# A decoder kernel on one core: setup joined to the main program, and in the 32-head stage the projections moved ahead of the scores and half of the softmax sums done by GpSimd

## The reference

```python
def _L3_attn_ref(x, w_qkv, w_out, b_out, ln_gamma, ln_beta):   # HEADS = 32, DIM_HEAD = 32
    qkv = (x @ w_qkv).reshape(b, n, 3, HEADS, DIM_HEAD).transpose(2, 0, 3, 1, 4)
    q, k, v = (qkv[0], qkv[1], qkv[2])
    dots = jnp.einsum('bhnd,bhmd->bhnm', q, k) * 32 ** (-0.5)
    attn = jax.nn.softmax(dots, axis=-1)
    out = jnp.einsum('bhnm,bhmd->bhnd', attn, v).transpose(0, 2, 1, 3).reshape(b, n, 1024)
    out = out @ w_out + b_out           # then a layer norm with ln_gamma and ln_beta
```

## Time and profile before

| What | Value |
|---|---|
| median of three runs | 1448.85 us |
| the profiled execution, its time | 1460.55 us |
| its span, from first to last instruction | 1458.7 us |
| mean granted TensorE clock | 0.927 |
| PE busy | 1230.4 us (84%) |
| DVE busy | 918.5 us (63%) |
| ACT busy | 649.7 us (45%) |
| POOL busy | 170.3 us (12%) |
| chain that ended last, PE's share | 70% |

### The profile page before, as it was taken

The page is one execution under the profiler, slowest core; times in us unless marked ns, Lnnn a source line. Parts: engine busy times, 40 slices in busy tenths (PEclk is TensorE's granted clock), DMA queues, the critical chain, the costliest instruction groups (busy, mean ns, idle before and its releaser), DMA issues.

```text
span 1458.7 us, 27476 instructions
## 1 busy us (share of the span) xinstructions
PE 1230.4 (84%) x10752; PEld 858.3 (59%) x10752; DVE 918.5 (63%) x2432; ACT 649.7 (45%) x1253; POOL 170.3 (12%) x242
## 2 busy tenths in 40 slices
PE   2489999999999999997888998787879986898751
PEld 1356766776676767775555676454556564556530
DVE  2463453536786878877775877975875446544557
ACT  2134345445544554456543446442436643554320
POOL 3221021102200200020000120000030001000011
PEclk9589999999999999998997999997989999999975
DMA  7001110111021102110000010000000000000000
GB/s 273 1 1 44 44 30 17 57 51 52 10 64 51 52 1 73 30 30 1 2 1 1 2 37 1 1 2 1 2 1 2 1 2 2 1 2 1 2 0 29
DMA packets 23143, 35.59 MB, mean 24 GB/s; under 512 B 4568, under 2 KB 12904, under 8 KB 22760
## 3 DMA queue, kind: packets, MB, share of 16 engines
q1 hardware_dynamic: 23016, 33.83, 7.5%
HBM read 32.77 MB, written 1.05 MB: 23 GB/s over the span
## 4 chain that ended last, share of the span: by engine, by line
PE 70%; DVE 13%; ACT 8%; issue 6%; POOL 1%; DVEq 0%; ACTq 0%; POOLq 0%
PE banks L1187 12%; PE banks L1171 11%; PE banks L1925 5%; PE banks L1938 4%; PE banks L1946 3%; DVE arena L2066 2%; ACT XALL L535 2%; PE banks L1967 2%; PE banks L923 2%; PE banks L897 2%; PE banks L545 2%; PE banks L1920 2%; PE banks L661 2%; PE banks L1886 1%; PE banks L937 1%
## 5 line engine op out<-in xcount | busy, mean ns | idle before, releaser
L2066 DVE TENSOR_REDUCE arena<-banks 128x4 f32<-128x1024 f32 x128 | 151.1, 1219 | 106.1 <-PE banks L1902 106.0
L1187 PEld LDWEIGHTS banks<-WE,arena 128*128 128x128 f32 x1536 | 180.0, 192 | 24.4 <-issue 23.3
L1231 ACT ACTIVATE arena<-banks,BC 128x512 f32<-128x512 f32 x192 | 130.5, 688 | 120.2 <-PE banks L1171 119.9
L1187 PE MATMUL banks<-WE,arena 128*128 128x128 f32 x1536 | 182.3, 276 | 0.0
L1171 PE MATMUL banks<-XT,WE 128*128 128x512 f32 x384 | 179.0, 602 | 0.0
L2044 ACT ACTIVATE arena<-banks 128x1024 f32<-128x1024 f32 x128 | 126.4, 1022 | 112.2 <-PE banks L1925 111.5
L1271 DVE SCALAR_TENSOR_TENSOR R<-banks,arena,R 128x128 f32<-128x128 f32 x256 | 71.9, 343 | 111.2 <-PE banks L1187 110.9
L1925 PE MATMUL banks<-arena 32*128 32x256 f32 x1024 | 112.7, 396 | 0.0
L579 ACT COPY arena<-banks 128x512 f32<-128x512 f32 x108 | 61.3, 591 | 115.2 <-PE banks L574 35.8
L1171 PEld LDWEIGHTS banks<-XT,WE 128*128 128x128 f32 x384 | 69.2, 192 | 69.1 <-issue 67.6
L1741 DVE TENSOR_TENSOR arena<-arena 128x512 f32<-128x512 f32 x144 | 100.8, 700 | 3.8
(11 more groups left out here) (305 smaller groups left out, 2149.4 us busy)
## 6 DMA issues: line engine op xcount, KB each, us to landing
WE<-in_weights SPq DMA_DIRECT2D x64, 256.0 KB, 2.9
WE<-in_weights SPq DMA_DIRECT2D x64, 128.0 KB, 2.2
WS<-in_weights SPq DMA_DIRECT2D x1, 2368.0 KB, 13.2
RW<-in_rows SPq DMA_DIRECT2D x1, 1032.0 KB
XALL<-in_x SPq DMA_DIRECT2D x4, 256.0 KB, 10.8
out_dram<-arena SPq DMA_DIRECT2D x4, 256.0 KB, 2.3
WS<-in_weights SPq DMA_DIRECT2D x1, 900.0 KB, 7.9
WS<-in_weights SPq DMA_DIRECT2D x1, 645.0 KB, 8.0
```

What stands on the lines that cost most here:

```text
L1187: ins = PE.matmul(v[:, tile(t)], self.HT[:, e % 2, j, tile(t)], self.W[:, (8 * i + e) % RING, 1, j], start=j == 0, stop=j == self.J - 1)
L1231: A.activation(self.HT[:, e % 2, j], psum.view(f"{self.L}.h{i}.{e}.{j}"), ACT.Relu, bias=bcol(self.p + "_b1", e * self.J + j))\
L2066: V.tensor_reduce(big.mx[:, 2 * pair:2 * pair + 2], v, AX.X, ALU.max, negate=True).then_inc(dve.read(f"big.m{i}.{n}.{pair}"), 1)
```

## The change

1. The setup functions become `setup_sp`, `setup_pool`, `setup_act` and `setup_dve`, called at the head of the main block's programs. What the end of the first block assured is now waited for by semaphores: PE waits for `setup_step` 23 before its first transposes and for `heads_made` 15 before `x0`, POOL for `heads_made` 15 after its own setup, DVE for `setup_step` 31 before the first decay product. The first weight DMA (645 KB) is split: the four weights of the first projections alone under `w_loaded[0]`, the rest under `small_loaded`.
2. In `big`, project(n+2) stands ahead of scores(n) and not project(n+3) behind values(n-1); ACT's copies(n+2) stand ahead of the exponentials of group n.
3. GpSimd adds the exponentials of the second key block to those of the first, in place, for groups 0 to 14 of each chunk: 60 additions of 128x1024 elements. PE's sum matmuls (`sums`) of those groups then cover one key block. They stand one slot later than before, between project(n+2) and scores(n) as sums(n-2), and wait for the addition. The addition itself waits for the product with v, which reads what it overwrites. Group 15 keeps both key blocks. Inversion, spreading and output of the first batch come one slot later.
4. `TURNS` is a new string. The lengths of the stages are the same.

```diff
 TURNS = (
-    "00000000000000010010101000101011011010101010112021022010012202021021200121010021101202101201320323031121023012"
+    "00000000000000010010011000101011101010101010110212102200212012120021210010210200101202101203102011021211230203"
...
-        with nc.Block(no_gpsimd_drain=True) as block:
-            @block.sync
-            def _(sp):
-                sp.dma_start(XALL[:, 0:4], x[:, 0:4]).then_inc(x_loaded[0], 16)
-                load_group(sp, 0)
+        def setup_sp(sp):
+            sp.dma_start(XALL[:, 0:4], x[:, 0:4]).then_inc(x_loaded[0], 16)
+            sp.dma_start(WS[:, 0:4 * D], weights[:, 0:4 * D]).then_inc(w_loaded[0], 16)
+            sp.dma_start(WS[:, 4 * D:GROUP_AT[1]], weights[:, 4 * D:GROUP_AT[1]]).then_inc(small_loaded, 16)
...
@@ big_pe
-                if n % 8 == 0:
-                    psum.take(pe, f"big.sum{i}.{n // 8}")
-                v = psum.view(f"big.sum{i}.{n // 8}")
-                for kt in range(2):
-                    for h in range(4):
-                        ins = PE.matmul(v[32 * h:32 * h + 32, 0:S], group_column[:, n % 8].rearrange("p a c -> p (a c)"),
-                                        big.E[:, n % 2, h, kt, :], start=n % 8 == 0 and kt == 0,
-                                        stop=n % 8 == 7 and kt == 1, skip_group_check=True)
...
+            def sums(n):
+                b, g = divmod(n, 8)
+                added = n < GROUPS - 1
+                if added:
+                    pe.wait_ge(sig("big.added"), (GROUPS - 1) * i + n + 1)
+                if g == 0:
+                    psum.take(pe, f"big.sum{i}.{b}")
+                v = psum.view(f"big.sum{i}.{b}")
+                for kt in range(1 if added else 2):
+                    for h in range(4):
+                        ins = PE.matmul(v[32 * h:32 * h + 32, 0:S], group_column[:, g].rearrange("p a c -> p (a c)"),
+                                        big.E[:, n % 2, h, kt, :], start=g == 0, stop=g == 7 and (added or kt == 1),
+                                        skip_group_check=True)
...
             for n in range(GROUPS + 1):
                 if n + 1 < GROUPS:
                     maxima(n + 1)
+                if n + 2 < GROUPS:
+                    project(n + 2)
+                if n >= 2:
+                    sums(n - 2)
                 if n < GROUPS:
                     scores(n)
                 if n >= 1:
                     values(n - 1)
...
-                if n + 3 < GROUPS:
-                    project(n + 3)
                 if n + 1 < GROUPS:
                     shifts(n + 1)
@@ big_act
             for n in range(GROUPS + 1):
+                if n + 2 < GROUPS:
+                    copies(n + 2)
...
-                if n + 3 < GROUPS:
-                    copies(n + 3)
@@ big_pool
-            yield from idle(GROUPS + 2)
+            for n in range(GROUPS + 1):
+                if 1 <= n < GROUPS:
+                    pool.eng.wait_ge(*psum.made(f"big.o{i}.{n - 1}"))
+                    E = big.E[:, (n - 1) % 2]
+                    G.tensor_tensor(E[:, :, 0], E[:, :, 0], E[:, :, 1], ALU.add).then_inc(pool.flag("big.added"), 1)
+                yield
+            yield
@@ main block
             @block.tensor
             def _(eng):
+                eng.wait_ge(setup_step, 23)
                 run(0, lambda i: eng)
...
             @block.vector
             def _(eng):
+                setup_dve(eng)
```

More of the change, by code:

```diff
@@ new lines, in setup_sp @@
+        def setup_sp(sp):
+            sp.dma_start(XALL[:, 0:4], x[:, 0:4]).then_inc(x_loaded[0], 16)
+            sp.dma_start(WS[:, 0:4 * D], weights[:, 0:4 * D]).then_inc(w_loaded[0], 16)
+            sp.dma_start(WS[:, 4 * D:GROUP_AT[1]], weights[:, 4 * D:GROUP_AT[1]]).then_inc(small_loaded, 16)
+            sp.dma_start(BC[:], bcols).then_inc(small_loaded, 16)
+            sp.dma_start(RW[:], rows.partition_broadcast(P)).then_inc(small_loaded, 16)
+            sp.dma_start(B2[:], b2s.rearrange("l e d -> e l d")).then_inc(small_loaded, 16)
+            sp.dma_start(CD[:], ctx_d).then_inc(loaded, 16)
+            sp.dma_start(KEEP0[:], keep0.partition_broadcast(P)).then_inc(loaded, 16)
+            sp.dma_start(KEEP3[:], keep3.partition_broadcast(P)).then_inc(loaded, 16)
+            for half in range(2):
+                keys = slice(64 * half, 64 * half + 64)
+                with nc.allow_non_contiguous_dma(reason="the masks, keys on partitions"):
+                    sp.dma_start(KEEPC0[keys], keep0.rearrange("b k -> k b")).then_inc(loaded, 16)
+                    sp.dma_start(KEEPC3[keys], keep3.rearrange("b k -> k b")).then_inc(loaded, 16)
+            sp.dma_start(XALL[:, 4:8], x[:, 4:8]).then_inc(x_loaded[1], 16)
+            for e in range(RING):
+                load_expert(sp, 0, e)
+            load_group(sp, 3)
+            for e in range(RING):
+                load_expert(sp, 1, e)
+            load_group(sp, 5)
+            load_group(sp, 6)
+            for i in range(2, CHUNKS):
+                sp.dma_start(XALL[:, 4 * i:4 * i + 4], x[:, 4 * i:4 * i + 4]).then_inc(x_loaded[i], 16)
@@ L738, in ret_dve @@
                 if k < PAIRS:
+                    if i == 0 and k == 0:
+                        dve.eng.wait_ge(setup_step, 31)
                     dve.eng.wait_ge(*psum.made(f"ret.s{i}.{k}"))
@@ L841, in pe @@
                 L = self.L
+                pe.wait_ge(heads_made, 15)
                 pe.wait_ge(loaded, LOADS * 16)
-                pe.wait_ge(w_loaded[self.group], 16)
+                if self.group:
+                    pe.wait_ge(w_loaded[self.group], 16)
+                else:
+                    pe.wait_ge(small_loaded, 64)
                 v = psum.take(pe, f"{L}.k{i}")
@@ L1948, in values @@
                 ins.then_inc(psum.filled(f"big.o{i}.{n}"), 1)
+            def sums(n):
[11 more added lines that the diff above has]
+                                        skip_group_check=True)
+                if g == 7:
+                    ins.then_inc(psum.filled(f"big.sum{i}.{b}"), 1)
             def spread(b, pairs):
@@ L1985, in big_pe @@
                     values(n - 1)
-                if n in (9, 10):
-                    spread(0, (2 * n - 18, 2 * n - 17))
-                if n == 11:
+                if n == GROUPS:
+                    sums(n - 1)
+                if n in (10, 11):
+                    spread(0, (2 * n - 20, 2 * n - 19))
+                if n == 12:
                     output(0)
-                if n + 3 < GROUPS:
-                    project(n + 3)
                 if n + 1 < GROUPS:
@@ L2034, in big_act @@
             yield
-            copies(2)
             shift_copy(0)
```

193 lines of the change are left out of this document (87 added, 106 removed).

## The result

The changed kernel takes 1468.24 us (median of 4 runs, 1466.81 to 1468.63), the kernel before 1448.56 (now four runs, 1442.31 to 1449.97). The ratio is 1.0126, with a 95% interval of 1.0076 to 1.0176: it is slower by some 18 us, where 1408 was forecast, with a range of 1378 to 1440. The prediction was wrong in sign. The profiled execution took 1467.89 us, its span is 1466.1, and the mean granted clock fell from 0.927 to 0.910.

A forecast was written before the change was run, and what follows sets the result against it. The prediction took TensorE, busy 84% of the span, as the bound. Its terms, -15.2 - 30 - 14 + 13 + 5 = -41.2 us, took the median 1448.85 to 1407.6, forecast as 1408 with a range of 1378 to 1440.

The forecast's parts named there:

- Setup, -15.2: At the start, PE's first transposes begin at 7.4 and not at 22.64 us, a gain of 15.2 us.
- Rival B: Only the setup gains, as waits for the addition and DVE stops eat the rest: 1434 us, chance 0.15.
- Half the sums, -30: In `big`, 60 groups each save 0.50 us of PE's sum matmuls: 30.0 us, with 15 as lower bound.
- Projections and copies ahead, -14: In lone groups of `big`, PE's 1.49 us wait for ScalarE's copies goes: 31 pairs at 0.45 us, 14 us gained.
- The addition, 2.55 and a wait of 0.6: GpSimd's 1024-element addition takes about 2.55 us, 2.6 with semaphores, and PE's sums wait 0.6 in a lone group.
- The lock, +13: GpSimd additions reading SBUF stop DVE's two-operand sorting steps beside groups: up to 30 us, taken as 13 for slack.
- +5 for neighbouring groups: In the new list, 9 more neighbouring pairs of groups each pay the uncovered 0.6 us wait: 5 us lost.
- Queued behind waits, within the order's bounds: Waits of PE and GpSimd hold other chunks' work, layer norms starting up to 2.6 us later; given no separate size.
- The new order, 0 with 15 on either side: How well the new list of turns interleaves can't be read off; bounded by 15 us either way.
- A: Slower: additions stop DVE in sort slots and other stages, delaying the maxima PE waits for: 1470 us, chance 0.08.

The follow-up runs named there:

- full sums: The changed kernel without GpSimd's additions, PE summing both key blocks of every group; 1418.64 us, ratio 0.9789 to the kernel before.
- unused additions: 60 additions of 128x1024 on the no longer used decay table, nobody waiting, put into full sums; 1450.31 us, ratio 0.9989 to the kernel before.
- setup alone: The kernel before with only the setup joined, old list of turns and old body of `big`; 1447.93 us, ratio 0.9925.
- short additions: The changed kernel with each addition 64 elements wide, same waits and flags, not computing the reference; 1410.72 us, ratio 0.9735 to the kernel before.
- the last version above: The changed kernel with additions only for groups 0 to 11 of chunks 2 and 3; 1411.63 us, ratio 0.9712 to the kernel before.

## Why the prediction was wrong, step by step

By the ratios, the 18 us can be put together so: setup -11, projections and copies moved -4.5, new list with the new body -15 (together full sums, -30.5), half the sums -8, lock +29, ends of the chunks +25. That sums to +15.5; measured are +18.3. The last three are differences of single experiments, so this is a reckoning to some 5 us and not to one. That it comes so near is in part luck: the 29 were measured with unused additions, where DVE is busy 29.2 more, and in the changed kernel DVE is busy only 22.6 more, so its own lock may be nearer to that; and the 25 are net of eight groups' halved sums.

*Setup, -15.2.* The mechanism and its time in the timeline were right (7.46 against 7.4). The ratio of setup alone gives -11, and its interval, 5 to 16, doesn't exclude 15.2. Rival B's 1434 rests on the same term.

*Half the sums, -30.* This term was mis-sized, and it is the first step that failed: "All of it lies on PE. I take the whole, -30". PE does have 28.8 us less of them. But with short additions the whole gives 8 us over full sums. Where a group stands alone the saving is nearly whole: the period from scores to scores is 5.97 in the changed kernel (below) and 6.40 in full sums, whose timeline has

```profile
1077.37 0.39 PE L1924 MATMUL banks<-arena,ones 32*128 32x512 bf16 x2
...
1083.78 0.39 PE L1924 MATMUL banks<-arena,ones 32*128 32x512 bf16 x2
...
1090.18 0.39 PE L1924 MATMUL banks<-arena,ones 32*128 32x512 bf16 x2
```

That is 0.43 less for 0.50, and the last version above, with halved sums in 24 groups of chunks 2 and 3, gains 11 us. With short additions and 60 halved groups it is 8, so the other groups gave nothing that can be seen. In the kernel with short additions the sums take 26.7 us less than in full sums (43.0 for 69.7), but PE's other work takes 14.6 more, at a mean granted clock of 0.929 for 0.941, and the sums wait 5.0 for GpSimd. In the changed kernel the clock was 0.910. My lower bound was 15, and even that was too high.

*Projections and copies ahead, -14.* The second term that failed. The chain's wait of 1.49 did go, as said. But the next one wasn't GpSimd's addition. A lone group of chunk 2 in the changed kernel:

```profile
1132.69 0.39 PE L1924 MATMUL banks<-arena,ones 32*128 32x512 bf16 x2
...
1135.30 2.48 POOL L2147 TENSOR_TENSOR arena<-arena 128x1024 f32<-128x1024 f32 x1 [3.63 <-PE banks L1940]
...
1135.84 2.36 DVE L2078 TENSOR_REDUCE arena<-banks 128x4 f32<-128x1024 f32 x2 [0.26 <-PE banks L1906]
...
1136.05 0.39 PE L1906 MATMUL banks<-arena 32*128 32x256 bf16 x4 [0.32 <-ACT arena L2058]
1136.13 0.41 ACT L2042 COPY arena<-banks 128x256 f32<-128x256 f32 x1
...
1136.59 0.70 PE L1890 MATMUL banks<-XT,WS 128*128 128x256 f32 x2
...
1138.09 0.64 PE L1954 MATMUL banks<-arena,group_column 128*32 128x256 f32 x8
...
1138.66 0.39 PE L1924 MATMUL banks<-arena,ones 32*128 32x512 bf16 x2
```

The addition ends at 1137.78 and the sums start at 1138.09: nobody waits for it. Nor does it stop the two maxima beside it, 2.36 for both. PE now waits for ScalarE in two places that I counted as free. The second maxima at 1136.05 start when the second exponentials of L2058 release their bank, and the projection at 1136.59 when ScalarE's copy L2042 ends at 1136.54. I had added up ScalarE's work, "some 4.0, less than PE", and took it as hidden; what counts is that its exponentials and copies stand between PE's matmuls in the order in which the banks come free. The period without the additions is 6.40, against 6.45 before: 0.05 and not 0.45. In the whole kernel it gives 4.5 us on the old list, within the noise of nothing.

*The addition, 2.55 and a wait of 0.6.* It took 2.35 alone (median 2346 ns), so scaling up from 256 and 512 elements overrated it. The Trainium skill, "GPSIMD Engine Reference" (Elementwise, side-by-side cycle accounting), states 4497 ns for 2048 elements. Half of that, an estimate of 2.25, is the nearer one. The wait in a lone group was 0, and before group 12 PE waited 2.6 us in all for additions, so +5 for neighbouring groups was too much.

*The lock, +13.* The mechanism was read rightly from one row, and the case of 12 sort slots at 2.5 each, "If each is stopped once in full and DVE decides there, the cost is 12 x 2.5 = 30", is about what came: 29 with the unused additions, where twelve sorting steps were stretched, 2.0 us each and not 2.5, and shorter instructions beside them. The step that failed is the discount, "some of it falls in slack". I took the slack from DVE's busy share, 70 to 75% of the stretch. That share says nothing of the moment: the maxima, for which PE waits, stand behind the stopped step in DVE's own queue, as at 927.85. In the changed kernel ten stops were seen, close to the 12 that the prediction gave as the least.

*Queued behind waits, within the order's bounds.* That term was missing in fact. I named what waits behind GpSimd, and not what GpSimd's addition waits behind, and took a lone group for all groups of a chunk. At a chunk's end there is neither a projection nor a next group to cover the addition: +25.

*The new order, 0 with 15 on either side.* With the new body it gave -15, the edge of my bound; with the old body it costs some 41 (1.0208 against 0.9925). So neither can be priced without the other.

*The rivals.* A named the lock and gave 1470; the measured 1468 is near by chance. The lock alone is 29, half of the 61 at which A was to turn the sign. Setup, sums and projections gave 23.5 of the 59.2 that I had for them, and the list 15 more; the lock left 9.5 of these 38.5, and the chunks' ends, which no rival had, turned the sign. A and the ends are one kind of case, GpSimd's additions costing more than they save, and 0.08 was too little for it: no row bore out that any of the three gains would be seen in full.

What stays open: in what place the new list costs the old body its 41 us, which no trace here was read for; and why additions for groups 0 to 12 leave the stretch from 1037.5 to 1162.5 at 125.0 us and a clock of 0.89, where full sums takes 123.4 at 0.96 (its second measurement some 1 us more) and the changed kernel 118.5 at 0.97. How much of each difference is the clock itself and how much the waits that stand before it fell wasn't separated: no experiment held the clock fixed.

## What to carry to other kernels

A GpSimd instruction that reads SBUF, issued just before a VectorE instruction with two SBUF inputs, costs VectorE nearly its whole length (2.16 of 2.35 us here). Price it in full, once for each place where such work shares a stretch with it and something that is waited for stands behind in VectorE's queue, whatever VectorE's busy share says. Before work is handed to another engine, look at the ends of the pipeline too, where nothing covers it, and at what stands ahead of it in that engine's queue. And a list that was tuned to one body of code is part of that body: with the old one it cost 2.8%, with the new one and without additions it gave 1.0%.

## What the runs showed of the hardware

- Sixty GpSimd additions that read SBUF (2.35 us each) cost 29 us with nobody waiting for them, and another 60 that only write it (1.87 us each) cost nothing that could be told from the noise.
- A stopped sorting step ended 0.55 us behind the addition, both for an addition of 1.27 and for one of 2.35: it does nearly its whole work of 0.69 after the stop, whatever the stop's length.
- An addition that began 0.01 us behind a sorting step took 2.89 us in place of 2.35, and the sorting step its usual 0.69. Two maxima beside an addition, which read PSUM, took 2.36, their usual 1.2 each.
- In the half-clock stretch from 1208.4 to 1222.0 sixteen records of values took 1.93 us, and 1.07 at the full clock. It began within a wait of PE of 4.10 us that ended at 1209.70.
